# Second attention of a two-layer macaron block: scores in a ring of three pairs of banks, values two or three slots behind

## The chip, the cores and the metric

The kernel runs on one NeuronCore of one Trainium2 chip. The metric is device time in microseconds of one execution; lower is better. Engines are named as in the profile: PE is TensorE's matmuls (PEld its weight loads), DVE is VectorE, ACT is ScalarE, POOL is GpSimd, SP is the engine whose queue issues all DMAs. They run at the same time and meet at semaphores.

## What is computed

The input is 8 sequences of 512 tokens by 128 features. Two layers, each a feed-forward mixture of experts, an attention, and the same feed-forward again. The change touches the second layer's attention:

```python
def kernel_func(q, k):
    scores = jnp.einsum('bhqd,bhkd->bhqk', q, k) / jnp.sqrt(jnp.asarray(HD, q.dtype))
    w = jax.nn.relu(scores)
    return w / (jnp.sum(w, axis=-1, keepdims=True) + KERN_EPS)
...
qkv = (x @ w_qkv).reshape(Bx, Sx, H, 3 * HD)
...
attn = kernel_func(q, k)
out = jnp.einsum('bhqk,bhkd->bhqd', attn, v)
...
out = out @ w_out + b_out
y = x + out
```

There are 16 heads of 8 features. There is no mask and no exponential: the weights are relus, divided by their sum. A layer norm over the features of y ends it. The attention's input `x` is itself a layer norm of the running x, and what comes out is added to the running x.

## The kernel before, in words

Everything is float32 (or float32r, split in a high and a low part where three products replace one). The program runs six stages (`STAGES`): ffn0, attn0, ffn0, ffn1, attn1, ffn1. Each takes the eight sequences, called blocks here (`Chunk` in the code), one after the other; the first and the last block are written out, the six between are one loop body. A block has slots: 16 in attn1 (`NS1`). The order on every engine is written by hand. In each slot `run` issues first the steps of the block before that are left (`TAIL`: half, fin, aT_hi, aT_lo, proj, y_norm, y_rstd, y_scale, y_add), then steps that prepare the next block (`PREP`: the layer norm, its turn on PE, hi and lo; `QKV_AT`: keep, q, q_hi, q_lo, k, k_hi, k_lo, v, v_out), then the slot's own work. A number in these tables is the slot in which a step stands.

In attn1 a slot n is one group of four heads (quad, n // 4) and one block of 128 keys (n % 4). Its own work is:

- PE (`pe_attn1`, L753): four score matmuls (L763), one for each head of the quad. Each uses 24 rows of a strip of 32, so the four run beside each other. Each writes its own bank (0 to 3), 128 keys by 512 queries. Matmul j waits until the relu of slot n-1 for strip j is done (`p1_ready[j]`). Then come the four values matmuls of slot n-1 (`pv1`, L589, L598), float32, each to a strip of 32 output rows; the trace shows eight records for them. They add up over eight slots (two quads) in bank 5 for the first half of the heads and in bank 6 for the second.
- ACT (L881) and DVE (L1156) turn the scores into weights by a relu of 128x512 out of PSUM into the ring `probs` of three slots. ACT takes strips 0 and 1, and in slots 0, 2, 4, 6, 8, 10 strip 3 too; DVE takes the others.
- After eight slots the half of the output is turned and divided on DVE (`take_half`, L1063: L1075 transposes, L1081 adds the epsilon, L1083 takes the reciprocal, L1087 multiplies). The first half's stands in DVE's slot 9, ahead of the relus; the second half's in slot 1 of the next block.
- POOL copies the values into place (`put_values`, L1243), adds the last layer-norm bias to x (L1249, slot 10) and does the two steps of y_add (L1223, L1226), 128x512 each.
- SP writes q's and k's parts to DRAM (`write_stacks`) and reads them back for the four quads (`read_stacks`) in the layout of strips. A quad's buffers may be overwritten once its last score matmul of this block is done.

The steps that prepare the next block all use bank 7; the projection of the block before used bank 4 (`tail_bank`).

## Time and profile before

| | us |
|---|---|
| median of 3 runs | 2202.41 (2200.76 to 2204.6) |
| the profiled execution | 2207.97, its span 2206.2 |
| second attention in that span | 1484.0 to about 1812 |
| mean granted TensorE clock, whole span | 0.969 |

The profile is one execution. Its page gives the busy time of each engine, the trace behind it each instruction's start and duration, and what released an engine that had been idle. Matmul ends are modelled, so PE's busy time is read with care; starts are better. The granted clock is 1.00 at 2.4 GHz and 0.50 at 1.2 GHz; a stretch with both shows a mean.

### The profile page before, as it was taken

The page shows a single profiled execution, that of the slowest core. Times are in us where ns is not written, and L with a number is a line of the kernel's source. Part 1 is how long each engine was busy: PE and PEld are TensorE (multiplying, and loading weights), DVE is VectorE, ACT ScalarE, POOL GpSimd, SP SyncE. Part 2 cuts the span into 40 slices and gives each one's busy share as a digit, 9 for nine tenths or more (in the row PEclk, how much of TensorE's full clock was granted, in tenths as well). Part 3 has the DMA queues.
Part 4 walks back from the last instruction along what each step waited for, and adds up shares of the span by engine and source line. Part 5 has one row for each costly group of instructions (what it writes and reads, how often), then busy time and mean ns, then how long its engine had stood idle before and what let it go on. Part 6 is the DMA issues. An engine that isn't in the chain of part 4 may idle for free.

```text
span 2206.2 us, 45682 instructions
## 1 busy us (share of the span) xinstructions
PE 2073.0 (94%) x10800; PEld 1467.0 (66%) x10800; DVE 1683.5 (76%) x3458; ACT 1198.0 (54%) x1873; POOL 925.4 (42%) x904
## 2 busy tenths in 40 slices
PE   2999998999999899999999999999899899999999
PEld 2777776666666677777777777763333237777777
DVE  3777777777777577777588888876777777888887
ACT  3666664555555566666444444445555554444444
POOL 1655554323332456666444444440211214444444
PEclk9999998999999999999999999998889799999999
DMA  4333334233332234434211111123223201111112
GB/s 159 108 101 111 107 105 125 79 100 100 86 86 76 79 116 113 119 116 118 76 44 44 43 43 47 46 90 99 93 76 107 83 30 39 44 43 43 43 42 74
DMA packets 119983, 179.36 MB, mean 81 GB/s; under 512 B 33408, under 2 KB 37856, under 8 KB 119776
## 3 DMA queue, kind: packets, MB, share of 16 engines
q1 hardware_dynamic: 119904, 178.41, 27.0%
q8 instruction: 36, 0.59, 0.1%
q14 instruction: 43, 0.35, 0.0%
...
## 4 chain that ended last, share of the span: by engine, by line
PE 60%; issue 14%; POOL 11%; DVE 10%; ACT 2%; DMA 1%; SPq 1%; DVEq 1%; POOLq 1%; ACTq 0%
PE pair L382 12%; PE pair L384 11%; PE pair L383 11%; POOL h_lo L1282 9%; PE pair L763 4%; PE bank L598 3%; PE pair L598 3%; PE pair L683 3%; PE bank L584 3%; PE pair L705 3%; PE bank L382 1%; DVE rmax L1112 1%; PE bank L384 1%; PE bank L383 1%; DVE h_hi L1055 1%
## 5 line engine op out<-in xcount | busy, mean ns | idle before, releaser
L1288 POOL TENSOR_TENSOR h_lo<-hid,h_hi 128x512 fp32r<-128x512 f32 x256 | 333.7, 1303 | 441.5 <-ACT h_hi L852 441.4
L382 PE MATMUL pair<-xnT_hi,w_hi 128*128 (+1 forms) x1056 | 432.9, 410 | 1.1 <-DVE prod L1035 1.1
L1282 POOL TENSOR_TENSOR h_lo<-hid,h_hi 128x512 fp32r<-128x512 f32 x256 | 329.9, 1292 | 225.5 <-ACT h_hi L820 224.3
L384 PE MATMUL pair<-xnT_hi,w_lo 128*128 (+1 forms) x1056 | 418.4, 396 | 0.0
L383 PE MATMUL pair<-xnT_lo,w_hi 128*128 (+1 forms) x1056 | 416.2, 394 | 0.0
L847 ACT ACTIVATE hid<-pair,bias 128x512 f32<-128x512 f32 x256 | 176.3, 689 | 326.8 <-PE pair L384 323.0
L382 PE MATMUL pair<-h_hi,w_hi 128*128 128x512 f32 x784 | 318.3, 406 | 18.4 <-POOL h_lo L1282 8.9
L384 PE MATMUL pair<-h_hi,w_lo 128*128 128x512 f32 x784 | 309.5, 395 | 0.0
L383 PE MATMUL pair<-h_lo,w_hi 128*128 128x512 f32 x784 | 308.5, 394 | 0.0
L1055 DVE TENSOR_SCALAR h_hi<-pair,nb 128x512 fp32r<-128x512 f32 x256 | 191.1, 747 | 84.2 <-PE pair L384 83.2
L1035 DVE SCALAR_TENSOR_TENSOR prod<-pair,bias,wb 128x512 f32<-128x512 f32 x256 | 191.0, 746 | 67.0 <-PE pair L384 56.1
L870 ACT ACTIVATE probs<-pair 128x1024 f32<-128x1024 f32 x160 | 163.5, 1025 | 129.5 <-PE pair L705 126.1
L382 PEld LDWEIGHTS pair<-xnT_hi,w_hi 128*128 128x128 f32 x1056 | 199.9, 189 | 49.5 <-issue 6.1
L820 ACT ACTIVATE h_hi<-hid 128x512 fp32r<-128x512 f32 x256 | 161.2, 630 | 130.5 <-DVE hid L1040 126.2
L384 PEld LDWEIGHTS pair<-xnT_hi,w_lo 128*128 128x128 f32 x1056 | 199.2, 189 | 48.3
L881 ACT ACTIVATE probs<-pair 128x512 f32<-128x512 f32 x304 | 163.5, 598 | 121.3 <-PE pair L763 114.5
L383 PEld LDWEIGHTS pair<-xnT_lo,w_hi 128*128 128x128 f32 x1056 | 200.3, 190 | 39.1
L1040 DVE TENSOR_TENSOR hid<-pair,prod 128x512 f32<-128x512 f32 x256 | 177.1, 692 | 55.1 <-DVE prod L1035 35.7
L826 ACT ACTIVATE pair<-pair,bias 128x512 f32<-128x512 f32 x256 | 167.6, 655 | 72.6 <-PE pair L384 69.7
L1057 DVE SCALAR_TENSOR_TENSOR h_lo<-pair,nb,h_hi 128x512 fp32r<-128x512 f32 x256 | 192.2, 751 | 9.1
L1267 POOL TENSOR_SCALAR_AFFINE_SELECT probs<-probs 128x512 f32<-128x512 f32 (+1 forms) x160 | 86.9, 543 | 266.2 <-ACT probs L870 266.2
L382 PEld LDWEIGHTS pair<-h_hi,w_hi 128*128 128x128 f32 x784 | 147.8, 189 | 70.4 <-DVE h_lo L1057 11.3
...
## 6 DMA issues: line engine op xcount, KB each, us to landing
wb<-parts_dram SPq DMA_DIRECT2D x512, 128.0 KB, 2.9
wb<-parts_dram SPq DMA_DIRECT2D x128, 256.0 KB, 3.3
...
k_one<-parts_dram SPq DMA_DIRECT2D x128, 64.0 KB, 2.4
...
```

The costliest lines, as they stand in the source:

```text
L382: eng.matmul(o, w_hi_, v_hi, start=start, stop=False, **kw)
L383: eng.matmul(o, w_hi_, v_lo, start=False, stop=False, **kw)
L384: return eng.matmul(o, w_lo_, v_hi, start=False, stop=stop, **kw)
L826: eng.activation(gate_bank(p)[:, :] if p else gate[:, :], gate_bank(p)[:, :], ACT.Silu, bias=bias[:, b:b + 1]).then_inc(silu_ready, 1)
L847: eng.activation(hid[:, i % NHID, :], unit_bank(j)[:, :], ACT.Relu, bias=bias[:, B1 + j:B1 + j + 1]).then_inc(hid1_ready, 1)
L870: eng.activation(probs0[:, fill, :, :], pair[ring(("k", n))][:, :, :], ACT.Exp).then_inc(p0_full, 1)
L1035: eng.scalar_tensor_tensor(prod[:, p % 2, :], bank[2 + p % 2][:, :], bias[:, b:b + 1], wb[:, i % NWB, :], ALU.add, ALU.mult).then_inc(prod ...
L1040: eng.tensor_tensor(hid[:, i % NHID, :], gate_bank(p)[:, :], prod[:, p % 2, :], ALU.mult).then_inc(hid_ready, 1)
L1055: eng.tensor_scalar(h_hi[:, j % NH1, :], unit_bank(j)[:, :], floor, None, ALU.max).then_inc(hi1v_ready, 1)
L1057: eng.scalar_tensor_tensor(h_lo[:, j % NH1, :], unit_bank(j)[:, :], floor, h_hi[:, j % NH1, :].bitcast(F32), ALU.max, ALU.subtract).then_i ...
L1282: eng.tensor_tensor(h_lo[:, p % NH0, :], hid[:, unit_of(p) % NHID, :] if p else hs[:, :], h_hi[:, p % NH0, :].bitcast(F32), ALU.subtract). ...
L1288: eng.tensor_tensor(h_lo[:, j % NH1, :], hid[:, j // 2 % NHID, :], h_hi[:, j % NH1, :].bitcast(F32), ALU.subtract).then_inc(lo1p_ready, 1)
```

## The change

1. **Pairs.** The scores of a slot are now two pairs, m = 2n (strips 0 and 1) and 2n+1 (strips 2 and 3). Pair m is written to the two-bank tile `pair[m % 3]`, so banks 0 to 5 are a ring of three. A relu takes a whole pair, 128x1024. ACT takes each first pair, and in slots 0, 2, 10, 11, 13 (`ACT_BOTH`) the second too: 21 of 32. DVE takes 11. There is one counter for each of the two engines (`p1_ready`).
2. **Both waits, then four matmuls.** In slot n PE waits for the relus of the pairs three back, 2n-3 and 2n-2, and then issues the four score matmuls with no wait between.
3. **Values behind.** `PV_AT` lists which values steps stand in which slot. Slot 0 has step 13 of the block before, slot 1 its 14 and 15, slot 2 none, slot 3 steps 0 and 1, then n-2 up to slot 9, slot 10 none, and from slot 11 on n-3. All sums go to bank 6, so step 0 waits for the second half of the block before to be turned out of it, step 8 for the first half of this one. The ring of probs has four slots.
4. **Places.** half, fin, aT_hi, aT_lo move one slot back (2, 3, 4, 5), the first half's take from slot 9 to 10, the projection from 6 to 10 (now in bank 7), y_norm to 11, y_rstd 12, y_scale 13, y_add 14. q moves from slot 4 to 6, k from 5 to 7, v from 7 to 8, keep from 11 to 15. The layer norm's steps move by at most one slot, those of routing (last block) by up to two.
5. **Memory.** The larger probs ring lies over the buffer of the spread routing weights, so the loads for the stage after wait until the last values step (`pv1_done`); `attn1_xk` moves to buffers that only the first layer uses.

The core of the diff:

```diff
-    ("attn1", "attn1"): ((0, "pe", "pv_last"), (1, "dve", "half"), (2, "dve", "fin"), (3, "act", "aT_hi"),
-                         (4, "dve", "aT_lo"), (6, "pe", "proj"), (7, "dve", "y_norm"), (8, "pool", "y_rstd"), (9, "dve", "y_scale"), (10, "pool", "y_add")),
+    ("attn1", "attn1"): ((2, "dve", "half"), (3, "dve", "fin"), (4, "act", "aT_hi"), (5, "dve", "aT_lo"), (10, "pe", "proj"),
+                         (11, "dve", "y_norm"), (12, "pool", "y_rstd"), (13, "dve", "y_scale"), (14, "pool", "y_add")),
...
-    "attn1": (11, 4, 4, 4, 5, 5, 5, 7, 7),
+    "attn1": (15, 6, 6, 6, 7, 7, 7, 8, 8),
...
-HEAD_ORDER = (0, 2, 1, 3)
-ACT_THIRD = (0, 2, 4, 6, 8, 10)
+PV_AT = ((-3,), (-2, -1), (), (0, 1), (2,), (3,), (4,), (5,), (6,), (7,), (), (8,), (9,), (10,), (11,), (12,))
+ACT_BOTH = (0, 2, 10, 11, 13)
...
+def taken_by(m):
+
+    return "act" if m % 2 == 0 or m // 2 in ACT_BOTH else "dve"
...
             if kb == 0 and quad % 2 == 0:
-                eng.wait_ge(o_turned, 2 * ch.ga - 1 + quad // 2)
+                eng.wait_ge(o_turned, 2 * ch.ga + quad // 2)
+            for h in range(2):
+                eng.wait_ge(*taken_wait(ch, 2 * n + h))
             for j in range(QUAD):
-                eng.wait_ge(p1_ready[j], ROUND + i + 1)
-                ins = eng.matmul(bank[5 + quad // 2][PC * j:PC * (j + 1), :], mem1.v_st[:, kb, quad, j, :],
+                ins = eng.matmul(bank6[PC * j:PC * (j + 1), :], mem1.v_st[:, kb, quad, j, :],
...
-            for j in HEAD_ORDER:
-                rows_ = slice(PC * j, PC * j + NROW * HD)
-                eng.wait_ge(p1_ready[j], ROUND + i)
-                eng.matmul(bank[j][:, :], mem1.k_st[rows_, quad, kb * P:(kb + 1) * P], mem1.q_st[rows_, quad, :],
-                           start=True, stop=True).then_inc(s1_ps, 1)
-            if n:
-                pv1(eng, ch, n - 1)
+            for h in range(2):
+                m = 2 * n + h
+                if m >= NPAIR or not ch.first:
+                    eng.wait_ge(*taken_wait(ch, m - NPAIR if m >= NPAIR else max(k for k in range(NP1) if k % NPAIR == m) - NP1))
+            for h in range(2):
+                m = 2 * n + h
+                for j in range(2):
+                    rows_ = slice(PC * (2 * h + j), PC * (2 * h + j) + NROW * HD)
+                    ins = eng.matmul(pair[m % NPAIR][:, j, :], mem1.k_st[rows_, quad, kb * P:(kb + 1) * P], mem1.q_st[rows_, quad, :],
+                                     start=True, stop=True)
+                ins.then_inc(s1_ps, 1)
+            for m in PV_AT[n]:
+                if m >= 0:
+                    pv1(eng, ch, m)
+                elif not ch.first:
+                    pv1(eng, ch.before(), m + NS1)
...
+            elif before is not None and before.kind == "attn1":
+                eng.wait_ge(pv1_done, ROUND + NB * NS1)
```

How the order changes at three places of the middle blocks' body. ISA and REGISTER_ALU rows only wait or compute a semaphore's value. First PE, around the half. Before, the scores of slot 9 and the start of values step 8, with a wait at each matmul (pair0 and pair1 are banks 0 to 3):

```order
L763 MATMUL pair0<-attn1_q_st,attn1_k_st 128x512 [waits p1_ready0]
L762 ISA
L763 MATMUL pair1<-attn1_q_st,attn1_k_st 128x512 [waits p1_ready2]
L762 ISA
L763 MATMUL pair0<-attn1_q_st,attn1_k_st 128x512 [waits p1_ready1]
L762 ISA
L763 MATMUL pair1<-attn1_q_st,attn1_k_st 128x512 [waits p1_ready3]
L593 ISA
L595 ISA [waits v_put]
L597 ISA [waits o_turned]
L598 MATMUL bank6<-probs,attn1_v_st 32x512 [waits p1_ready0]
```

After, slots 10 and 11 (pair0 to pair2 are the ring; slot 10 has no values), up to the waits of values step 8:

```order
L777 ISA [waits p1_dve_ready]
L782 MATMUL pair2<-attn1_q_st,attn1_k_st 128x512 [waits p1_act_ready]
L782 MATMUL pair2<-attn1_q_st,attn1_k_st 128x512
L782 MATMUL pair0<-attn1_q_st,attn1_k_st 128x512 x2
L777 ISA
L777 ISA [waits p1_dve_ready]
L782 MATMUL pair1<-attn1_q_st,attn1_k_st 128x512 [waits p1_act_ready]
L782 MATMUL pair1<-attn1_q_st,attn1_k_st 128x512
L782 MATMUL pair2<-attn1_q_st,attn1_k_st 128x512 x2
L603 ISA
L607 ISA [waits v_put]
L609 ISA [waits o_turned]
```

The four waits became two, the values matmuls between the two slots' scores are gone, and the wait for the turned half stands ahead of step 8.

DVE at the same place. Before, slot 9, from the last op of y_scale to the last of the half (the relus of slot 9 follow it):

```order
L1199 TENSOR_SCALAR attn1_xk<-attn1_xk,y_mv,y_rstd 128x128
L1070 ISA
L1072 ISA [waits pv1_done]
L1075 STREAM_TRANSPOSE attn1_o_turn<-pair2 128x512 [waits attn_ready]
L1076 ISA
L1081 TENSOR_SCALAR rden<-attn1_o_turn 128x32 [waits o_turned]
L1082 ISA
L1083 RECIPROCAL rden<-rden 128x32 [waits eps_added]
L1084 ISA
L1086 REGISTER_ALU [waits rden_ready]
L1087 TENSOR_TENSOR attn1_attn<-attn1_o_turn,rden 128x16x16 [waits aT_ready]
```

After, slot 10, from the relu of slot 9 on; y_norm of slot 11 follows:

```order
L1180 TENSOR_SCALAR probs<-pair1 128x1024 [waits s1_ps]
L1094 ISA
L1096 ISA [waits pv1_done]
L1099 STREAM_TRANSPOSE attn1_o_turn<-bank6 128x512 [waits attn_ready]
L1100 ISA
L1105 TENSOR_SCALAR rden<-attn1_o_turn 128x32 [waits o_turned]
L1106 ISA
L1107 RECIPROCAL rden<-rden 128x32 [waits eps_added]
L1108 ISA
L1110 REGISTER_ALU [waits rden_ready]
L1111 TENSOR_TENSOR attn1_attn<-attn1_o_turn,rden 128x16x16 [waits aT_ready]
```

The half no longer follows y_scale; it stands between a relu and y_norm (L1210 and on), and no relu follows for two slots.

POOL in the middle body. Before, y_add (L1223, L1226), released by y_scale, and behind it the bias op L1249:

```order
L1221 ISA
L1223 ISA [waits tail_steps]
L1223 ISA
L1223 TENSOR_TENSOR attn1_xk<-attn1_xk,row 128x512
L1225 REGISTER_ALU [waits y_scaled]
L1226 ISA [waits x_biased]
L1226 ISA x2
L1226 TENSOR_TENSOR x<-x,attn1_xk 128x512
L1248 ISA
L1249 ISA [waits ln_steps]
L1249 ISA
L1249 TENSOR_TENSOR x<-x,row 128x512
```

After, from the bias op (now L1274) over a values copy and y_rstd to y_add (L1248, L1251):

```order
L1274 TENSOR_TENSOR x<-x,row 128x512
L1265 ISA
L1268 COPY attn1_v_st<-attn1_v_tok 128x4x4x8 [waits pv1_done]
L1244 TENSOR_TENSOR y_rstd<-y_ve,mhalf 128x4 [waits y_var]
L1246 ISA
L1248 ISA [waits tail_steps]
L1248 ISA
L1248 TENSOR_TENSOR attn1_xk<-attn1_xk,row 128x512
L1250 REGISTER_ALU [waits y_scaled]
L1251 ISA [waits x_biased]
L1251 ISA x2
L1251 TENSOR_TENSOR x<-x,attn1_xk 128x512
```

The bias op and the second values copy moved ahead of y_rstd; behind y_add there are only keep and one copy before the block ends.

## Rows read from the trace of the kernel before

**Rows 1.** Stretches: length; PE, PEld, DVE, ACT, POOL busy (count); clock, DMA, GB/s.

```profile
1484.00:1524.70 40.70, 37.17 (x215) 12.25 (x214) 25.02 (x52) 22.76 (x42) 4.36 (x6) 0.83 0.27 84
1524.70:1771.80 247.10, 227.48 (x1357) 81.41 (x1356) 181.62 (x397) 137.41 (x258) 49.40 (x60) 0.85 0.28 90
1771.80:1812.30 40.50, 36.70 (x224) 12.49 (x223) 30.69 (x84) 22.83 (x44) 6.25 (x6) 0.92 0.11 33
```

**Rows 2.** Groups of lines in one block, 1648.8 to 1688.4; busy, mean ns | idle.

```profile
L881 ACT ACTIVATE probs<-pair 128x512 f32<-128x512 f32 x38 | 20.4, 599 | 14.2 <-PE pair L763 14.2
L1156 DVE TENSOR_SCALAR probs<-pair 128x512 f32<-128x512 f32 x26 | 17.0, 685 | 6.3 <-PE pair L763 6.0
```

**Rows 3.** Timeline of PE in one block: start, us, engine, line, what, count.

```profile
1572.22 0.66 PE L512 MATMUL bank<-ident,xn 128*128 128x128 f32 x4
1572.80 0.50 PE L763 MATMUL pair<-attn_q_st,attn_k_st 24*128 24x512 f32 x4
...
1575.17 0.80 PE L763 MATMUL pair<-attn_q_st,attn_k_st 24*128 24x512 f32 x4
...
1580.71 0.51 PE L763 MATMUL pair<-attn_q_st,attn_k_st 24*128 24x512 f32 x4
...
1583.64 0.50 PE L763 MATMUL pair<-attn_q_st,attn_k_st 24*128 24x512 f32 x4
...
1588.83 0.50 PE L763 MATMUL pair<-attn_q_st,attn_k_st 24*128 24x512 f32 x1
1591.91 1.24 PE L763 MATMUL pair<-attn_q_st,attn_k_st 24*128 24x512 f32 x3 [2.58 <-DVE probs L1156]
...
1594.94 0.80 PE L763 MATMUL pair<-attn_q_st,attn_k_st 24*128 24x512 f32 x4
...
1597.53 0.80 PE L763 MATMUL pair<-attn_q_st,attn_k_st 24*128 24x512 f32 x4
...
1599.86 0.50 PE L763 MATMUL pair<-attn_q_st,attn_k_st 24*128 24x512 f32 x4
...
1603.19 0.50 PE L763 MATMUL pair<-attn_q_st,attn_k_st 24*128 24x512 f32 x4
1603.63 2.53 PE L598 MATMUL bank<-probs,attn_v_st 128*32 128x512 f32 x16
1606.09 0.50 PE L763 MATMUL pair<-attn_q_st,attn_k_st 24*128 24x512 f32 x4
```

**Rows 4.** Timelines of DVE and of POOL around 1588 to 1592, same block.

```profile
1588.25 0.99 DVE L1081 TENSOR_SCALAR rden<-attn_o_turn 128x32 f32<-128x32 f32 x1
...
1589.76 1.50 DVE L1087 TENSOR_TENSOR attn_attn<-attn_o_turn,rden 128x256 f32<-128x256 f32 x1
1591.17 0.68 DVE L1156 TENSOR_SCALAR probs<-pair 128x512 f32<-128x512 f32 x1
...
1587.92 1.28 POOL L1223 TENSOR_TENSOR attn_xk<-attn_xk,row 128x512 f32 x1 [2.19 <-DVE attn_xk L1199]
1589.71 1.26 POOL L1226 TENSOR_TENSOR x<-x,attn_xk  x1 [0.51 <-POOL attn_xk L1223]
```

**Rows 5.** Stretches of the same block before, in and after a fall.

```profile
1589.30:1592.70 3.40, 0.81 (x4) 0.44 (x3) 3.28 (x5) 0.78 (x2) 2.99 (x4) 1.00 0.00 0
1592.70:1596.20 3.50, 3.50 (x17) 0.69 (x20) 0.83 (x2) 1.45 (x3) 1.14 (x1) 0.50 0.00 0
1599.50:1603.00 3.50, 3.50 (x28) 1.05 (x24) 2.61 (x5) 2.17 (x4) 0.29 (x1) 0.99 0.00 0
```

**Rows 6.** ACT's timeline, and 128x1024 ops of the first attention (groups by form).

```profile
1600.39 1.08 ACT L881 ACTIVATE probs<-pair 128x512 f32<-128x512 f32 x2 [0.95 <-PE pair L763]
...
L870 ACT ACTIVATE probs<-pair 128x1024 f32<-128x1024 f32 x17 | 17.4, 1025 | 14.3 <-PE pair L705 14.0
...
L1115 DVE TENSOR_REDUCE rmax<-pair 128x2 f32<-128x1024 f32 x7 | 8.6, 1222 | 2.6 <-PE pair L692 2.5
```

**Rows 7.** Timeline of SyncE's DMA queue, same block.

```profile
1583.24 0.34 SPq L1317 DMA_DIRECT2D attn_q_st<-parts_dram  x1
```

More of the change, by code:

```diff
@@ L183, in __init__, with taken @@
             self.rmax = sb("rmax", [P, 2, NT, QUAD], F32)
-        else:
-            self.xk = sb("attn1_xk", [P, 2, NT, D], F32)
-def act_heads(n):
-    return (0, 1, 3) if n in ACT_THIRD else (0, 1)
+def taken_by(m):
+    return "act" if m % 2 == 0 or m // 2 in ACT_BOTH else "dve"
+def taken(m, who):
+    return sum(taken_by(i) == who for i in range(m))
 def build(nc, x_in, w0, w1, wa, biases, bd3, rows, consts, out, scratch, mixed):
@@ L298, in build @@
         st_ready, p0_full, p0_masked, pv0_done = map(sem, ("st_ready", "p0_full", "p0_masked", "pv0_done"))
[L299 removed]
+        s1_ps, pv1_done = sem("s1_ps"), sem("pv1_done")
+        p1_ready = {"act": sem("p1_act_ready"), "dve": sem("p1_dve_ready")}
         o_turned, eps_added, rden_ready, attn_ready = map(sem, ("o_turned", "eps_added", "rden_ready", "attn_ready"))
@@ L435, in xs_of @@
             return x[:, bass.ds(ch.c * NT, NT), :]
-        def tail_bank(ch):
-            return bank[4] if ch.kind == "attn1" and not ch.last else bank7
         def gate_bank(k):
@@ L528, in pe_prep @@
                 eng.wait_ge(st.sem, ch.g * st.per + st.per)
+                if ch.first and ch.s and STAGES[ch.s - 1] == "attn1":
+                    eng.wait_ge(tail.sem, 13 * (NB - 2) + 1)
                 for t in range(NT):
@@ L587, in pv0, with taken_wait @@
             ins.then_inc(pv0_done, 1)
+        def taken_wait(ch, m):
+            who, back = taken_by(m % NP1), 0 if m >= 0 else 1
+            return p1_ready[who], ROUND + (ch.g - back) * taken(NP1, who) + taken(m % NP1 + 1, who)
         def pv1(eng, ch, n):
@@ L620, in pe_tail @@
             if step == "pv_last":
-                pv1(eng, ch, NS1 - 1)
+                for m in PV_AT[0] + PV_AT[1]:
+                    pv1(eng, ch, m + NS1)
             if step == "pv_2":
@@ L625, in pe_tail @@
                 eng.wait_ge(aT_lo_ready, ch.ga + 1)
-                if ch.kind == "attn1" and not ch.last:
-                    eng.wait_ge(x_done, ONE + ch.G)
+                if ch.kind == "attn1" and isinstance(ch.c, int) and ch.c == NB - 2:
+                    eng.wait_ge(aff_ready, ch.gf + 1)
                 elif ch.last or ch.causal and isinstance(ch.c, int) and ch.c == NB - 2:
@@ L877, in act_attn1 @@
             eng.wait_ge(pv1_done, ROUND + i - PRING + 1)
-            for j in HEAD_ORDER:
-                if j in act_heads(n):
-                    eng.wait_ge(s1_ps, i * QUAD + HEAD_ORDER.index(j) + 1)
-                    eng.activation(probs[:, n % PRING, j, :], bank[j][:, :], ACT.Relu).then_inc(p1_ready[j], 1)
+            for m in (2 * n, 2 * n + 1):
+                if taken_by(m) == "act":
+                    eng.wait_ge(s1_ps, ch.g * NP1 + m + 1)
+                    eng.activation(probs[:, n % PRING, 2 * (m % 2):2 * (m % 2) + 2, :], pair[m % NPAIR][:, :, :], ACT.Relu).then_inc(
+                        p1_ready["act"], 1)
         def dve_prep(eng, step, ch):
@@ L1070, in take_half @@
                 eng.wait_ge(pv1_done, ROUND + ch.g * NS1 + (2 * half + 2) * NT)
-                src = bank[5 + half]
+                src = bank6
             eng.wait_ge(attn_ready, n)
@@ L1152, in dve_attn1 @@
             eng.wait_ge(pv1_done, ROUND + i - PRING + 1)
-            for j in HEAD_ORDER:
-                if j not in act_heads(n):
-                    eng.wait_ge(s1_ps, i * QUAD + HEAD_ORDER.index(j) + 1)
-                    eng.tensor_scalar(probs[:, n % PRING, j, :], bank[j][:, :], 0.0, None, ALU.max).then_inc(p1_ready[j], 1)
+            for m in (2 * n, 2 * n + 1):
+                if taken_by(m) == "dve":
+                    eng.wait_ge(s1_ps, ch.g * NP1 + m + 1)
+                    eng.tensor_scalar(probs[:, n % PRING, 2 * (m % 2):2 * (m % 2) + 2, :], pair[m % NPAIR][:, :, :], 0.0, None,
+                                      ALU.max).then_inc(p1_ready["dve"], 1)
         def dve_tail(eng, step, ch):
@@ L1403, in dma_body @@
                         read_stacks(eng, after, g)
-            elif after is not None and after.kind[:4] == "attn":
+            if ch.kind != "attn0" and after is not None and after.kind[:4] == "attn":
                 write_stacks(eng, after)
```

38 lines of the change are left out of this document (21 added, 17 removed), and 2 rows, old and new, of the table PREP.

## Prediction

> **What bounds the kernel now.** The change touches the second attention alone, so I first cut the trace there. The table by stretches [rows 1] gives its three parts: the first block of 512 tokens 40.7 us, the six in the middle 247.1 us (41.2 each), the last 40.5 us up to its last slot. The reader is to see that no engine is full in the middle ones: per block DVE is busy 30.3 us, ACT 22.9, POOL 8.2. PE reads 37.9, but its granted clock is 0.85 there, and its records are long where it waits. So the block is set by how the engines hand over to each other, and by the clock. The groups of lines [rows 2] say what is handed over: 38 relus of 128x512 on ACT (20.4 us) and 26 on DVE (17.0 us, 685 ns each).
>
> Then the timeline of PE, read by the starts of L763, the four score matmuls of a slot [rows 3]. A slot's PE work at full clock is short: scores at 1603.19, values from 1603.63, so 0.43 us for scores; two values steps and the loop's end take the 2.46 us up to 1606.09, so about 1.0 us for a values step and 0.4 for the branch. A slot needs 1.45 us of PE, the slot with q 2.37 (1572.80 to 1575.17), the one with v 2.93 (1580.71 to 1583.64). Over a block that is 16x1.45, plus 0.6 for the turn (1572.22 to 1572.80), 2x0.9 for q and k, 2x1.35 for v and the projection: 28.3 us of 41.2. The rest is in few places. Scores 10 begin at 1588.83 with one strip; the other three wait until 1591.91, released by DVE's relu, and the next slot starts at 1594.94: 6.1 us for one slot. The reason is in the rows of DVE and POOL [rows 4]: DVE takes the first half's output between two of its relus; its 128x32 op L1081 takes 0.99 us while POOL's L1223 runs, and its L1087 1.50 us, ending 0.28 us after POOL's L1226. After such a stall the granted clock is 0.50, its level of 1.2 GHz, against 1.00 before (PE was busy 0.81 us of the 3.4 ahead of the fall [rows 5]), and slots take 2.59 us (1594.94 to 1597.53) until it is back.
>
> The Trainium skill, SBUF — State Buffer, section "Who interferes with whom", says that a DVE instruction in a two-port mode or with two SBUF inputs shares a port with GpSimd and that the second one blocks. By that rule the trace agrees: 0.99 and 1.50 us, while the relu at 1591.17, which reads PSUM, takes its usual 0.68 though POOL works beside it.
>
> **The change, part by part.**
>
> *Scores in three pairs.* Before, a strip's scores n+1 wait for that strip's relu n, and each engine does two or three relus in a row, so the fourth strip waits for the second or third relu. After, scores n+1 wait for pair 2n (always ACT's) and pair 2n-1 (a slot older). The loop is: score start to relu start, relu, relu end to next scores. The first is 0.53 us (1599.86 on PE, 1600.39 on ACT [rows 3, 6]). The relu of 128x1024 isn't in this stage; the nearest row is ACT's 128x1024 exponential out of the same pairs, 1025 ns [rows 6]. Bounds: 0.96 (two of the 0.48 by which ACT's relus follow each other, 1.08 us for two [rows 6]) to 1.20 (two of 599 ns). I take 1.03, since shape and source are the same. The hand-back I take as 0.05 (DVE's relu ends at 1591.85 [rows 4], the scores that waited for it start at 1591.91). Together 1.61 us per plain slot, against PE's 1.45.
>
> *Relus.* Back to back, ACT's 38 at 0.48 are 18.2 us; the new 21 at about 0.90 (1.03 less the same overlap of 0.12) are 19.0, with its other ops of about 3 us 22. DVE goes from 17.0 to 11 of 128x1024; the nearest row is its maximum over the same shape, 1222 ns [rows 6]; two relus of now are 1.37, and below the maximum I know no row: 13.4 us, so 30.3-17.0+13.4 = 26.7, less 2.2 if the blocked ops of [rows 4] run free. Both stay under the 32 us below.
>
> *Values two or three slots behind, four probs buffers.* The PE work is the same 16 steps, but no values step waits for the newest relu, and in slots 2 and 10 PE runs none, so the half can leave bank 6 meanwhile. If that cover is gone, values wait for the transpose of 0.7 us and the relus before it. Slots 1 and 3 have two steps and cost 0.43+2.0 = 2.43 each.
>
> *The half moved to slot 10, y_add to slot 14.* On DVE, slots 10 and 11 (and 0, 2, 13) have no relu any more, so half, y_norm and y_scale stand where ACT takes both pairs. POOL's two 1.27 us ops now stand behind y_scale of slot 13, when DVE does relus out of PSUM. The x+bias op L1249 comes right after v, at my count 0.8 us ahead of the half.
>
> *q, k, v, later by two slots or less.* q to lo_cut to k: by cut durations of 0.6 and 0.7 us (ACT, DVE) k can start 1.5 us after q's end, about what scores and one values step take. SP's queue moves with it: its first stack read is at 1583.24 [rows 7], 8 us after q's scores slot began at 1575.17, so some 4 us after k's cut. In the new block k is cut about half way (16 of 32 us), so the first stacks are in by 24 us and are needed at 32. Hidden; the cover is 8 us. The loads of the next stage's weight rows now wait for the last values; their first user is 7 slots on. Hidden.
>
> **The sum, at full clock.** Starts of scores 0 to 15 and the next 0, each the later of PE's queue and the relu loop: 1.61, 2.43 (two values), 1.61, 2.43 (two values; turn and hi beside them), 1.61, 2.33 (q), 2.37 (k, waits q_lo), 2.91 (v, waits k_lo), 1.66 (v_out ahead of the relu), 2.78 (projection), 1.61, 1.81 and 1.82 (ACT has both pairs of 10 and 11), 1.62, 1.80 (both of 13), 1.60: 32.0 us, plus 0.3 of the branch that the loop doesn't cover: 32.3. By the same split the block of [rows 3] has 13.7 us in slots 4 to 9 against 13.7, 11.0 against 5.2 in 10 to 12, 6.2 against 5.3 in 13 to 15, and the rest against 8.1 in 0 to 3. So most of the gain is the stall and the half clock behind it.
>
> *The clock.* With eight score and sixteen values records in 3.5 us it stays at 0.99 to 1.00 [rows 5]. The new block has no stretch as empty as 0.81 of 3.4 us; the two free steps leave PE idle some 0.7 and 1.1 us. I count one short spell at half clock in a block, 1.5 us: 33.8. Bounds: none (32.3) and what the trace has now: a mean of 0.85 is 30% of the time at half speed, where the block's work, 52 us by rival 3, runs at 0.62 of the pace: 36.4.
>
> Middle blocks: 247.1-6x33.8 = 44.3. First block: it starts at half clock after the hand-over and has no tail work in it: 40.7 to 35, 5.7. Last: routing in place of q, k, v: 40.5 to 35, 5.5. At the exit three values steps stand ahead of the next stage in place of one: +1.5. Together 54 us of the profiled execution's 2207.97 (span 2206.2, and nothing around it changes), so 2154 there; the median of the runs is 5.6 lower, 2202.41, which gives **2148 us**.
>
> The Trainium skill, TensorE: Matmul & The Clock Gate, section "A second HAM failure mode: psum-queue depth-cycling", tells of a kernel that cycles PSUM banks, idles PE briefly between groups and so keeps falling back to the slow clock. This speaks against the change, and is the third rival. The trace bears it out only behind longer idle times.
>
> **Rivals.**
> 1. *The loop is longer than 1.61.* If scores in effect wait for the DVE pair too (0.53+1.22+0.05 = 1.80 each) and DVE's side work (half, fin, lo, aT_lo in slots 2 to 5) pushes that pair back, eight plain slots cost 0.2 to 0.5 more and slots 3 to 5 one us each: 36.5 to 37. Gain 6x4.5+8 = 35: 2167. For it: DVE is 80% full there. Against: its pair has a slot of slack.
> 2. *No change that can be told.* The clock losses of now (36.4), the relu at 1.20 (16x0.17 = 2.7) and the stall merely moved (POOL's bias op beside the half, 2 us): 41 us a block, about 2200.
> 3. *Slower: the clock stays low.* At half speed a slot is 2.59 [rows 3]; with q and k at 1.8 each, v and projection at 2.7 each and turn at 1.2 that is 52 us a block. A share f of the time at half speed makes it 32.3/(1-0.38f): the break-even of 41.2 is f = 0.57. At 0.75 it is 45 a block, 2202+8x4 = 2234. Against: PE's load rises to 28.3 of 33 us, and the clock held under such a load in [rows 5].
> 4. *Better:* clock full and 32.3 in all blocks: 2137.
>
> **Chances.** Forecast 0.55 (2141 to 2158), better 0.14, rival 1 0.23, rival 2 0.03, rival 3 0.05. The range leaves out rivals 2 and 3 and the ends of the better case: 2134 to 2173. A change under 0.2% can't be told from none in a measurement of this kernel; so faster 0.93, same 0.02, slower 0.05.
>
> **What would show it.** Right: blocks of 33 to 34.5 us; plain slots of 1.6 to 1.7; the relus near 1.03 and 1.22; L763's successor never waiting 2 us for DVE; L1081 and L1087's successors at their short times in slot 10; stage clock above 0.93. Wrong: blocks above 36 with score matmuls released by DVE; a clock under 0.85 in a stage without stalls; values waiting for the half (o_turned) in slot 3 or 11; scores waiting for a stack's DMA at slot 0.

## The result, and the profile after

The changed kernel takes **2153.65 us** (median of 4 runs, 2147.16 to 2157.78). The kernel before takes 2203.51 us beside it (4 runs, 2200.76 to 2208.39). The ratio is 0.9769, 95% interval 0.9738 to 0.9799: 50 us less, where the forecast was 2148 and the range 2134 to 2173.

The profiled execution took 2147.16 us, its span is 2145.4 and its mean granted clock 0.987. It is 6.5 us below the median of its runs; the profiled one of before is 4.5 above the median of its own. So the two spans lie 60.8 us apart and the medians 49.9. What follows explains the 60.8 of the traces, and comes back to the difference.

The stretches of the second attention, cut at the same places as [rows 1] (length; busy PE, PEld, DVE, ACT, POOL with counts; clock, DMA share, GB/s). The last one ends with the last values step, where the next stage's first matmul starts:

```profile
1484.70:1519.60 34.90, 28.60 (x195) 9.15 (x194) 20.52 (x33) 22.48 (x25) 4.35 (x6) 0.85 0.28 92
1519.60:1715.50 195.90, 174.54 (x1357) 60.28 (x1358) 150.38 (x308) 138.16 (x156) 48.87 (x59) 0.99 0.36 113
1715.50:1750.80 35.30, 31.32 (x244) 10.01 (x244) 26.18 (x72) 22.81 (x27) 6.93 (x8) 0.95 0.05 16
```

The middle went from 247.1 us to 195.9, its clock from 0.85 to 0.99. Of before, the last stretch to the same event is 1771.8 to 1811.5:

```profile
1771.80:1811.50 39.70, 35.90 (x221) 11.82 (x220) 29.99 (x83) 22.83 (x44) 6.25 (x6) 0.91 0.09 28
```

The rest adds nothing: from there to the span's end it is 2206.2-1811.5 = 394.7 us before and 2145.4-1750.8 = 394.6 after, and up to the stage it is 0.7 more. So 5.8 + 51.2 + 4.4 - 0.7 = 60.7 us, all of the difference of the spans.

A single middle block with no spell at half clock lasts 32.5 us, one with such a spell 33.3:

```profile
1552.10:1585.40 33.30, 30.31 (x230) 10.19 (x230) 25.07 (x52) 23.12 (x26) 8.56 (x11) 0.95 0.36 110
1585.40:1617.90 32.50, 28.84 (x227) 9.99 (x228) 25.02 (x52) 23.01 (x26) 8.03 (x11) 1.00 0.36 113
```

Groups of lines in the second of them, which answer to [rows 2] and [rows 6]. L904 is now ACT's relu, L1180 DVE's, L1105 and L1111 what L1081 and L1087 were:

```profile
L904 ACT ACTIVATE probs<-pair 128x1024 f32<-128x1024 f32 x21 | 20.5, 1027 | 6.2 <-PE pair L782 6.2
L1180 DVE TENSOR_SCALAR probs<-pair 128x1024 f32<-128x1024 f32 x11 | 13.4, 1217 | 4.0 <-PE pair L782 4.0
L782 PE MATMUL pair<-attn_q_st,attn_k_st 24*128 24x512 f32 x65 | 8.6, 495 | 4.0 <-ACT probs L904 2.9 <-DVE probs L1180 0.7
...
L1111 DVE TENSOR_TENSOR attn_attn<-attn_o_turn,rden 128x256 f32<-128x256 f32 x2 | 0.8, 424 | 0.2
L1105 DVE TENSOR_SCALAR rden<-attn_o_turn 128x32 f32<-128x32 f32 x2 | 0.4, 189 | 0.1
```

Both of DVE's ops of the half stand at their short times, 189 and 424 ns, and the scores wait 0.7 us for DVE in the whole block. The timeline of PE in the same block answers to [rows 3]: slots 4 and 5 (1593.33, 1594.95), then 10, 11 and 12 (1607.30, 1608.91, 1610.74). L782 is the scores, L611 the values:

```profile
1593.33 0.50 PE L782 MATMUL pair<-attn_q_st,attn_k_st 24*128 24x512 f32 x4
1593.76 1.06 PE L611 MATMUL bank<-probs,attn_v_st 128*32 128x512 f32 x8
1594.95 0.51 PE L782 MATMUL pair<-attn_q_st,attn_k_st 24*128 24x512 f32 x4
...
1607.30 0.51 PE L782 MATMUL pair<-attn_q_st,attn_k_st 24*128 24x512 f32 x4
1608.91 0.51 PE L782 MATMUL pair<-attn_q_st,attn_k_st 24*128 24x512 f32 x4 [1.11 <-ACT probs L904]
1609.35 1.07 PE L611 MATMUL bank<-probs,attn_v_st 128*32 128x512 f32 x8
1610.74 0.50 PE L782 MATMUL pair<-attn_q_st,attn_k_st 24*128 24x512 f32 x4 [0.33 <-ACT probs L904]
```

A plain slot is 1.62 us, by the starts of the scores. The four score matmuls always go together, and no slot is near the 6.1 us of [rows 3]. What PE waits for there is ACT: 0.33 us in slot 11, where ACT takes both pairs, 1.11 us in slot 10, which has no values. DVE and POOL at the same place, which answer to [rows 4]:

```profile
1606.11 0.71 DVE L1099 STREAM_TRANSPOSE attn_o_turn<-bank 128x512 f32<-128x512 f32 x1
1606.85 0.19 DVE L1105 TENSOR_SCALAR rden<-attn_o_turn 128x32 f32<-128x32 f32 x1
...
1604.00 1.27 POOL L1274 TENSOR_TENSOR x<-x,row 128x512 f32 x1
...
1613.97 1.28 POOL L1248 TENSOR_TENSOR attn_xk<-attn_xk,row 128x512 f32 x1 [2.18 <-DVE attn_xk L1224]
```

POOL's bias op has ended at 1605.27, 0.8 us ahead of the half, and y_add starts at 1613.97, long after it. The first stack read of the block stands in SyncE's queue at 1605.36, 20 us into the block, where [rows 7] had its own 18 us into it:

```profile
1605.36 0.34 SPq L1342 DMA_DIRECT2D attn_q_st<-parts_dram  x1
```

No score matmul of slot 0 waits for it.

### The profile page after: what moved, and what is told of

It reads as the page before. It is cut to its first block, busy times and chain, and to the rows that moved or that the text cites. A ratio compares the mean times of both kernels' runs of the same rounds, so it can differ in the third digit from the quotient of the medians.

```text
span 2145.4 us, 44900 instructions
## 1 busy us (share of the span) xinstructions
PE 2006.2 (94%) x10800; PEld 1441.4 (67%) x10800; DVE 1645.3 (77%) x3338; ACT 1197.4 (56%) x1737; POOL 925.7 (43%) x904
## 4 chain that ended last, share of the span: by engine, by line
PE 57%; issue 15%; POOL 12%; DVE 9%; ACT 5%; DMA 1%; SPq 1%; POOLq 1%; DVEq 0%; ACTq 0%
PE pair L389 12%; PE pair L391 12%; PE pair L390 12%; POOL h_lo L1307 9%; PE bank L611 3%; ACT probs L904 3%; PE pair L697 3%; PE pair L719 3%; PE bank L589 2%; PE pair L782 2%; PE bank L389 2%; DVE rmax L1136 1%; PE bank L391 1%; PE bank L390 1%; PE pair L706 1%
## 5 line engine op out<-in xcount | busy, mean ns | idle before, releaser
L893 ACT ACTIVATE probs<-pair 128x1024 f32<-128x1024 f32 x160 | 163.4, 1025 | 129.6 <-PE pair L719 126.3
L1081 DVE SCALAR_TENSOR_TENSOR h_lo<-pair,nb,h_hi 128x512 fp32r<-128x512 f32 x256 | 192.3, 751 | 9.1
L904 ACT ACTIVATE probs<-pair 128x1024 f32<-128x1024 f32 x168 | 164.6, 1026 | 59.6 <-PE pair L782 53.0
```

The lines of the kernel that those rows point to most:

```text
L904: eng.activation(probs[:, n % PRING, 2 * (m % 2):2 * (m % 2) + 2, :], pair[m % NPAIR][:, :, :], ACT.Relu).then_inc(p1_ready["act"], 1)
L1081: eng.scalar_tensor_tensor(h_lo[:, j % NH1, :], unit_bank(j)[:, :], floor, h_hi[:, j % NH1, :].bitcast(F32), ALU.max, ALU.subtract).then_i ...
```

## The experiments

Ten experiments: eight further kernels, and the changed kernel twice more (8 and 10). Each has runs of the kernel before beside it (medians 2202.6 to 2205.4). The changed kernel's own medians are 2153.65, 2152.03 (experiment 8) and 2153.11 (10); differences against it are taken from these. "Slot" lengths are differences of the starts of the score matmuls.

**1. The half and y_add alone.** The kernel before, with y_scale in slot 13 (it was 9), y_add in 14 (10) and keep in 15 (11), so that POOL's two ops no longer meet the half.

```diff
-... (8, "pool", "y_rstd"), (9, "dve", "y_scale"), (10, "pool", "y_add")),
+... (8, "pool", "y_rstd"), (13, "dve", "y_scale"), (14, "pool", "y_add")),
-    "attn1": (11, 4, 4, 4, 5, 5, 5, 7, 7),
+    "attn1": (15, 4, 4, 4, 5, 5, 5, 7, 7),
```

> The kernel before with one thing moved: y_scale from slot 9 to 13, y_add from 10 to 14 and, behind it on POOL, keep from 11 to 15. Four single score banks, values one slot behind and the half in slot 9 stay. Theory A (the loss in slots 9 to 12 was DVE's half standing behind y_scale and beside POOL's y_add, and the half clock behind it): L1081 at 0.19 us and L1087 at 0.42 in slot 9, the gap of PE before the last three score matmuls of slot 10 falls from 2.6 us to under 1, the clock no longer falls there, blocks of 36 to 37.5 us in place of 41.2, 25 to 35 us off the program. Theory B (the ring of pairs is what matters, places are secondary): blocks of 40 to 41, under 8 us off.

Measured: 2183.47 us (2179.35 to 2185.96), ratio 0.9901, interval 0.9879 to 0.9923: about 22 us below before, short of theory A's 25 to 35, though the blocks are as long as it said. DVE and PE in slot 9 and 10 of a block at full clock:

```profile
1658.15 0.19 DVE L1081 TENSOR_SCALAR rden<-attn_o_turn 128x32 f32<-128x32 f32 x1
...
1658.85 0.43 DVE L1087 TENSOR_TENSOR attn_attn<-attn_o_turn,rden 128x256 f32<-128x256 f32 x1
...
1658.79 0.50 PE L763 MATMUL pair<-attn_q_st,attn_k_st 24*128 24x512 f32 x1
1659.93 1.09 PE L763 MATMUL pair<-attn_q_st,attn_k_st 24*128 24x512 f32 x3 [0.65 <-DVE probs L1156]
```

The two ops fell from 0.99 and 1.50 us to 0.19 and 0.43, the wait ahead of the three scores from 2.58 to 0.65, and slot 10 from 6.1 to 3.2 us. A middle block is 37.1 us in the mean (222.6/6), with a clock of 0.94 in place of 0.85:

```profile
1523.00:1745.60 222.60, 213.64 (x1361) 80.47 (x1360) 169.88 (x398) 136.65 (x258) 49.40 (x60) 0.94 0.31 99
```

The edit also takes y_scale away from DVE's place ahead of the half, so a second cause has to be ruled out: that the half merely stood behind y_scale. The transposes that open the half, first before, then here, rule it out:

```profile
1587.50 0.72 DVE L1075 STREAM_TRANSPOSE attn_o_turn<-pair 128x512 f32<-128x512 f32 x1
...
1657.40 0.72 DVE L1075 STREAM_TRANSPOSE attn_o_turn<-pair 128x512 f32<-128x512 f32 x1 [1.03 <-PE pair L598]
```

Slot 9's scores start at 1587.25 before and at 1657.16 here, so the half starts 0.25 and 0.24 us behind them. Here DVE has been idle for 1.03 us and waits for the values. What differs is the two ops beside POOL: together 1.87 us longer before, and the wait ahead of the three scores 1.93 us longer.

So the meeting of DVE and POOL is the cause of the stall, and of much of the half clock behind it. It is less than half of the gain: a block at full clock is still 35.6 us here and 32.5 in the changed kernel. Nor was all the half clock of before behind this stall. In the block of [rows 3] the clock fell once more, behind slot 0, and there PE had waited only 0.68 us:

```profile
1566.61 1.48 PE L763 MATMUL pair<-attn_q_st,attn_k_st 24*128 24x512 f32 x4 [0.68 <-ACT probs L881]
...
1565.40:1568.80 3.40, 2.72 (x17) 1.23 (x16) 3.17 (x11) 2.56 (x5) 1.28 (x2) 1.00 0.21 78
1568.80:1572.20 3.40, 3.40 (x17) 0.55 (x12) 3.00 (x8) 1.80 (x4) 0.00 (x0) 0.50 0.00 0
```

Of some 72 us at half clock in the middle stretch of before, some 48 stand behind slot 10's stall and 24 behind slots 0 and 1. In this experiment they are 17 and 10: the clock still falls behind slot 10 in four of the six blocks, where theory A had it that it no longer does.

**2. The scores wait for the newest pair too.** The changed kernel with one more wait ahead of the scores of slot n, for the second relu of slot n-1. This takes away the slack of the ring and nothing else.

```diff
+            if n or not ch.first:
+                eng.wait_ge(*taken_wait(ch, 2 * n - 1))
```

> The changed kernel with one more wait: the scores of slot n also wait for the relu of the newest pair, 2n-1, as a ring two pairs deep would. Theory A (the slack of one slot hides DVE's other work, rival 1 of the prediction): plain slots rise from 1.62 to about 1.85 where DVE has nothing else, to 2.5 where ACT has both pairs, and in slots 1 and 3, where DVE's relu ends 3.4 to 3.7 us after the scores, to 3.5 and more; blocks of 40 to 42 us, 55 to 75 us more than the changed kernel, so the time of the kernel before. Theory B (the gain came from the places, the ring's third pair is worth the 0.2 us a slot of a longer relu): blocks of 34 to 35.5, 12 to 25 us more.

Measured: 2210.76 us (2206.28 to 2213.77), ratio 1.0021, interval 1.0010 to 1.0032: 57 us above the changed kernel, and above before too. A plain slot is 1.87 us. Slots 0, 2 and 10 are 2.53 and slots 11 and 13 are 2.8, since in these five ACT does both relus one behind the other and the scores wait for the second. PE, then ACT:

```profile
1651.71 0.51 PE L784 MATMUL pair<-attn_q_st,attn_k_st 24*128 24x512 f32 x4
...
1654.23 0.51 PE L784 MATMUL pair<-attn_q_st,attn_k_st 24*128 24x512 f32 x4 [1.02 <-ACT probs L906]
...
1652.24 1.94 ACT L906 ACTIVATE probs<-pair 128x1024 f32<-128x1024 f32 x2 [0.91 <-PE pair L784]
...
1530.20:1772.60 242.40, 199.35 (x1360) 63.66 (x1360) 152.26 (x308) 141.23 (x156) 49.85 (x60) 0.87 0.29 91
```

ACT and DVE are busy about as long as in the changed kernel (141.2 and 152.3 us against 138.2 and 150.4), but the middle stretch is 242.4 us in place of 195.9. The shortest block is 39.1 us and the longest 40.9; part of that is half clock, which is back at a mean of 0.87. Slots 1 and 3 came out shorter at full clock (2.69 and 2.29) than the 3.5 expected. So without the slot of slack the wider relus, the new places and the values behind gain nothing over before. The wait for a pair that is a slot old is what the gain stands on, with the relus shared out as they are. That condition matters: in the shortest block (39.1 us, 6.6 above a block of the changed kernel at full clock) the five slots in which ACT takes both pairs make up 4.9 of the 6.6. Scores that wait for the newest pair, with the relus shared out to suit that wait, were not run, so the 57 us are not the price of the ring's third pair in general.

**3. No free steps.** Values step 0 in slot 2 and 1 in slot 3; step 8 in slot 10 and none in slot 11.

```diff
-PV_AT = ((-3,), (-2, -1), (), (0, 1), (2,), (3,), (4,), (5,), (6,), (7,), (), (8,), (9,), (10,), (11,), (12,))
+PV_AT = ((-3,), (-2, -1), (0,), (1,), (2,), (3,), (4,), (5,), (6,), (7,), (8,), (), (9,), (10,), (11,), (12,))
```

> The changed kernel with values step 0 in slot 2 and 1 in slot 3 (before: none in 2, both in 3), and step 8 in slot 10, none in 11 (before: none in 10). Theory A (a free step pays only where the half is not yet turned when PE gets there): in slot 2 PE waits some 1.5 us for the turned half, slots 2 and 3 together take 5.2 us in place of 4.04; in slot 10 the half is turned (1606.82) before PE gets to the values (1607.73), so slots 10 and 11 stay at 3.45. In all 1.2 us a block, 8 to 11 us more. Theory B (both free steps are needed): 2 us a block or more, and a wait for the half in slot 10 too. Theory C (neither is needed): within 3 us.

Measured: 2164.75 us (2162.96 to 2168.23), ratio 0.9813, interval 0.9789 to 0.9837: 11 us above the changed kernel.

```profile
1560.96 0.51 PE L782 MATMUL pair<-attn_q_st,attn_k_st 24*128 24x512 f32 x4
1563.14 1.06 PE L611 MATMUL bank<-probs,attn_v_st 128*32 128x512 f32 x8 [1.68 <-DVE attn_o_turn L1099]
```

PE stands 1.68 us for the transpose of the half, behind xn and a relu on DVE. Slot 2 is 3.77 us in place of 1.62 and slot 3 is 1.67 in place of 2.42: 1.4 us a block, which makes 8.4 of the 11 us over six blocks; the rest goes with more half clock (slot 2 is 5.0 us in two blocks). Slots 10 and 11 stay at 1.62 and 1.83. There the projection stands ahead of the scores of slot 10 and makes slot 9 2.92 us long, 1.3 more than a plain one, and DVE's transpose runs beside it (1606.11 to 1606.82 above). The free step of slot 10 is not needed for the half.

**4. The projection in slot 11** (`proj_11`). If slot 10's free step leaves PE idle for 1.11 us, the projection can stand there.

```diff
-    ("attn1", "attn1"): (... (10, "pe", "proj"),
+    ("attn1", "attn1"): (... (11, "pe", "proj"),
```

> The changed kernel with the projection in slot 11 in place of 10, so that PE does its twelve matmuls (1.35 us) in the free step behind scores 10, where it waits 1.11 us for ACT. Theory A (PE's idle time in slot 10 can take it): slot 9 falls from 2.92 to 1.65, slot 10 rises from 1.62 to about 1.9; 1.0 us a block, 6 to 9 us less than the changed kernel. Theory B (y_norm, later by as much, pushes DVE's relu of slot 12 and the scores of 14): under 3 us less.

Measured: 2149.95 us (2145.79 to 2151.82), ratio 0.9748, interval 0.9727 to 0.9769: 2 to 4 us below the changed kernel, with runs that overlap its runs, so theory A's 6 to 9 did not come. Slots 9 and 10 are 1.62 and 1.92 us where they were 2.92 and 1.62: 1.0 us won, and slot 11 is 1.62 where it was 1.83. But slots 2 and 3 are 2.19 and 2.57, 0.7 lost, and in two blocks a spell at half clock stands there (3.9 and 4.3 us for slot 3):

```profile
1649.41 0.80 DVE L923 TENSOR_SCALAR ve<-mv 128x4 f32<-128x4 f32 x1
...
1653.18 0.65 PE L515 MATMUL bank<-ident,xn 128*128 128x128 f32 x4 [0.64 <-DVE xn L932]
```

y_norm, y_scale and so POOL's y_add and keep all come later, DVE's L923 now runs beside keep (0.80 us in place of 0.17; POOL's keep runs from 1648.91 to 1650.19), rstd starts behind it, and the turn of xn on PE waits 0.64 us.

**5. Relus of half the width.** Each relu of a pair as two of 128x512; the pairs, waits and order stay.

```diff
-                    eng.activation(probs[:, n % PRING, 2 * (m % 2):2 * (m % 2) + 2, :], pair[m % NPAIR][:, :, :], ACT.Relu).then_inc(
+                    eng.activation(probs[:, n % PRING, 2 * (m % 2), :], pair[m % NPAIR][:, 0, :], ACT.Relu)
+                    eng.activation(probs[:, n % PRING, 2 * (m % 2) + 1, :], pair[m % NPAIR][:, 1, :], ACT.Relu).then_inc(
```

> The changed kernel with each relu of 128x1024 as two of 128x512, the counter raised by the second. Ring, waits and places stay. Theory A (the width of a relu only sets the loop's length): on ACT 0.49+0.60 = 1.09 in place of 1.03, so plain slots 1.68 in place of 1.62 and slots where ACT has both pairs 2.0 in place of 1.83; 0.6 to 1.2 us a block, 5 to 10 us more. Theory B (the wide relu is what the gain rests on): blocks of 36 us and more, 25 us more.

Measured: 2159.51 us (2157.72 to 2163.06), ratio 0.979, interval 0.9766 to 0.9813: 6 to 7.5 us above the changed kernel. A plain slot is 1.68 us, one with both pairs on ACT 1.96 (1.83), a block at full clock 33.4.

```profile
1630.77 0.60 ACT L904 ACTIVATE probs<-pair 128x512 f32<-128x512 f32 x1 [0.84 <-PE pair L782]
1631.26 0.59 ACT L905 ACTIVATE probs<-pair 128x512 f32<-128x512 f32 x1
...
1631.90 0.51 PE L782 MATMUL pair<-attn_q_st,attn_k_st 24*128 24x512 f32 x4 [0.17 <-ACT probs L905]
```

Two narrow relus take 1.08 us from start to end (1630.77 to 1631.85), one wide 1.03: the 0.06 that a plain slot grew. The width is worth about a seventh of the 50 us.

**6. The bias op beside the half.** POOL's L1274 one slot later, in slot 11.

```diff
-            if slot == BIAS_AT:
+            if slot == (BIAS_AT if ch.causal else BIAS_AT + 1):
```

> The changed kernel with POOL's x+bias op (L1274, 1.27 us) in slot 11 in place of 10, so that it starts with the values copy behind it, beside DVE's half of slot 10. Theory A (the port is shared whatever the kernel, but here no relu stands behind the half): L1105 or L1111 in slot 10 takes up to 1.3 us in place of 0.19 and 0.42, y_norm ends up to 1.2 us later, and the slots of PE stay as they are: within 3 us of the changed kernel. Theory B (a blocked half costs its own length wherever it stands): 1 us a block, 6 to 10 us more.

Measured: 2150.06 us (2146.98 to 2153.68), ratio 0.9752, interval 0.9725 to 0.9778: no cost against the changed kernel, whose medians are 2152.0 to 2153.7.

```profile
1608.25 0.91 DVE L1105 TENSOR_SCALAR rden<-attn_o_turn 128x32 f32<-128x32 f32 x1
...
1607.84 1.28 POOL L1274 TENSOR_TENSOR x<-x,row 128x512 f32 x1
```

L1105 takes 0.91 us in place of 0.19 and ends at 1609.16, POOL's op at 1609.12. The first half of what [rows 4] showed is back: 0.72 us for L1105. L1111 keeps its 0.42, since only one op of POOL stands there and not two. PE's slots do not move (1.62, 1.83, 1.83). DVE has no relu in slots 10 and 11, and its relu of slot 12 starts 0.2 us later than in the changed kernel. So slots in which DVE has no relu hide a meeting of this size; whether they would hide the whole 1.87 us of before, with the distance to POOL's ops given up, was not run.

**7. The projection in slot 11 and y_scale in slot 12** (`proj_11_scale_12`). A try at mending 4.

```diff
-    ("attn1", "attn1"): (... (10, "pe", "proj"),
-                         (11, "dve", "y_norm"), (12, "pool", "y_rstd"), (13, "dve", "y_scale"), (14, "pool", "y_add")),
+    ("attn1", "attn1"): (... (11, "pe", "proj"),
+                         (11, "dve", "y_norm"), (12, "pool", "y_rstd"), (12, "dve", "y_scale"), (14, "pool", "y_add")),
```

> As proj_11, and y_scale in slot 12 ahead of DVE's relu in place of slot 13. In proj_11 the slots 9 and 10 gained 1.0 us, but POOL's chain y_add, keep, values copy, rstd ended 0.7 us later (rstd started 2.26 us into the block in place of 1.54), the layer norm's turn with it, and slots 2 and 3 gave 0.7 us back. Theory A (that chain starts with y_scale): rstd back at 1.54, slot 2 at 1.62, slot 3 at 2.42, blocks of 31.4 us where the clock is full; 6 to 9 us less than the changed kernel in all. Theory B (DVE's relu of slot 12, later by 1.2 us, holds the scores of slot 14): slot 13 above 2.2, nothing gained over proj_11.

Measured: 2158.32 us (2155.91 to 2158.6), ratio 0.9787, interval 0.9765 to 0.981. Slots 2 and 3 are 1.62 and 2.32 again, but slot 13 is 3.74 us:

```profile
1647.83 1.41 DVE L1224 TENSOR_SCALAR attn_xk<-attn_xk,y_mv,y_rstd  x4 [1.55 <-POOL y_rstd L1244]
1649.15 1.22 DVE L1180 TENSOR_SCALAR probs<-pair 128x1024 f32<-128x1024 f32 x1
...
1650.50 0.50 PE L782 MATMUL pair<-attn_q_st,attn_k_st 24*128 24x512 f32 x4 [2.24 <-DVE probs L1180]
```

The relu of slot 12 is now queued behind y_scale, which waits 1.55 us for POOL. Like the loss of before in slot 10, it is a relu behind side work on DVE; here the side work waits for a result of POOL, there it ran beside POOL's ops. The kernel is 5 to 6 us above the changed one, and theory B held.

**8. The changed kernel once more,** for the spread between executions.

> The changed kernel unchanged, to see how far its execution with a profile is typical: the one shown ran in 2147.2 us at a mean clock of 0.987, the others at 0.980 to 0.983 in 2153 to 2158. If the clock is the difference, this profile has the same slots of 1.62, 1.83, 2.3 to 3.0 us, and 2 to 5 more spells at half clock in some stage, each worth about 1.5 us; if something else is, the slots themselves differ.

Measured: 2152.03 us (2148.81 to 2153.3), ratio 0.9755, interval 0.9731 to 0.978. The slots at full clock are the same to 0.02 us in four of six middle blocks. The other two are 35.5 and 34.3 us, with half clock in slots 11 to 15, where the first profile had one such block (33.3). Its span is 2150.3 and its clock 0.984, against 2145.4 and 0.987.

**9 and 10. ACT takes slot 12's second pair in place of slot 13's,** with the projection in slot 11 (`proj_11_both_12`), and the changed kernel beside it.

```diff
-    ("attn1", "attn1"): (... (10, "pe", "proj"),
+    ("attn1", "attn1"): (... (11, "pe", "proj"),
-ACT_BOTH = (0, 2, 10, 11, 13)
+ACT_BOTH = (0, 2, 10, 11, 12)
```

> The projection stands in slot 11 as in proj_11, and ScalarE takes both relus of slot 12 instead of those of slot 13, so that VectorE has no relu between y_norm and y_scale. Theory A (what proj_11 lacked was the start of y_scale on VectorE: it stood behind the relu of slot 12, so that GpSimd's y_add, keep, copy and rstd all came 0.7 us late and the first slots of the next block waited): y_scale starts as soon as GpSimd's y_rstd is done, rstd starts about 1.5 us into the next block as in the changed kernel, slots 2 and 3 are 1.62 and 2.42 us again, slots 9 and 10 stay 1.62 and 1.92; a block is 31.4 us at full clock against 32.5, and the kernel 6 to 9 us below the changed one. Theory B (VectorE's relu of slot 13 now stands behind y_scale and ends late, as in proj_11_scale_12): the scores of slot 14 or 15 wait 0.5 to 1.5 us for it, a block is 32 to 33 us, and the kernel is within 3 us of the changed one or above it.

> The changed kernel unchanged, on the same chip and in the same rounds as proj_11_both_12. Both theories: the slots as in its profile (a block 32.5 us at full clock) and a median of 2148 to 2155 us; it tells what a difference of 3 to 6 us between the two is worth.

Measured: 2144.31 us (2143.17 to 2147.7), ratio 0.9719, interval 0.9699 to 0.9739, against 2153.11 us (2147.23 to 2154.4) of the changed kernel, ratio 0.975, interval 0.9728 to 0.9772. So 8.8 us less, the size that theory A gave, but only partly by its way. Slots 9 and 10 are 1.62 and 1.92, slot 2 is 1.64; but slot 3 is 2.57, slot 14 is 1.91 and slot 15 is 2.18 (1.83 and 1.87 before, theory B's cost). A block is 32.1 us, 0.4 less and not 1.1. The rest is the clock: the six middle blocks of the one and of the other are

```profile
1523.20:1715.80 192.60, 173.53 (x1360) 60.21 (x1360) 151.25 (x308) 138.63 (x156) 48.02 (x58) 1.00 0.36 115
...
1523.00:1722.90 199.90, 180.22 (x1356) 61.12 (x1356) 150.27 (x307) 138.42 (x156) 48.86 (x59) 0.96 0.35 110
```

7.3 us, of which 6x0.4 = 2.5 are the slots and 4.8 the half clock in three blocks of the second (34.4, 33.3, 34.6 against 32.5). Ahead of one of these falls, and behind it, the stretches of the changed kernel read

```profile
1612.80:1616.20 3.40, 1.97 (x20) 0.50 (x20) 2.54 (x11) 3.01 (x4) 0.08 (x1) 1.00 0.80 263
1616.20:1623.00 6.80, 6.80 (x36) 1.32 (x36) 3.14 (x6) 4.56 (x5) 3.65 (x4) 0.50 0.19 68
```

PE was busy 1.97 of 3.4 us, in which the free step of slot 10 falls. With the projection there it is busy 3.37 of 3.4 and then 3.06 of 3.5, and the clock stays:

```profile
1608.10:1611.50 3.40, 3.37 (x28) 1.96 (x28) 2.59 (x7) 2.83 (x3) 0.31 (x1) 1.00 0.85 268
1611.50:1615.00 3.50, 3.06 (x28) 0.70 (x24) 1.75 (x11) 3.50 (x5) 1.02 (x1) 1.00 0.59 190
```

In the changed kernel the same idle time stands in all six blocks and the clock fell behind it in one, two and three of them in three profiles. What decides between them stays open. That filling slot 10 keeps the clock up is what this profile without a fall in its middle blocks and the narrow range of five runs speak for. The profiles of experiments 4 and 7, which fill slot 10 too, agree: neither has a fall behind slot 10 in six blocks, only behind the waits in slot 2 (two blocks) and in slot 13. That makes none in 18 blocks, against six in the 18 of the three profiles of the changed kernel. In all of these traces a fall stands behind idle time of PE, but not every such idle time has a fall behind it.

## Why the prediction was right

The signs and the mechanism held, and the median fell in the forecast's own range (2141 to 2158). Step by step:

- **The loop.** Forecast 1.61 us for a plain slot, measured 1.62; relus 1.03 and 1.22, measured 1.027 and 1.217. That the maximum and the exponential of the first attention, taken as the nearest rows, cost just what the relus do was an assumption that held. The slots at full clock follow the list within 0.14 us each, but for slot 15, 1.87 against 1.60 (the 0.3 of the branch were added apart): 32.5 against 32.3 for a block. Slots 10 to 12 are 1.62, 1.83, 1.83 against 1.61, 1.81, 1.82. The largest other misses are 0.14 us: the projection's slot over, slot 1 under.
- **PE's own work** 28.8 us a block against 28.3, DVE 25.0 against 24.5, ACT 23.0 against 22.
- **The half.** L1105 and L1111 ran free as forecast, and experiment 1 shows the cause. The prediction put most of the gain there and on the half clock behind it; undone alone it gives 22 of 50 us. By experiment 2 the slack of a slot is worth 57 when all the rest is there. The two are taken from different ends, one from before and one from after, and are not a split of the 50. So the prediction's split is borne out only in part: more than half of the 50 needs the rest of the change, with the slack of the ring in it, though the prediction read the loop as a small gain beside the stall.
- **Free steps.** Right for slot 2 (1.4 us a block without it), wrong for slot 10: the projection covers the transpose there, and the free step costs 1.11 us of idle PE, and perhaps some of the clock (experiments 9 and 10).
- **Stacks and cover.** Read 20 us into the block, no wait.
- **The clock.** The mis-sized term. It was counted at 1.5 us a block, 9 for the six; in the three profiles it is 0.8, 4.8 and 4.8 in all six. The middle was put at 202.8 us and is 195.9 in the first of them. The prediction also read the trace of before as having falls only behind longer idle times, from the one behind 0.81 us of busy PE in 3.4. That reading is wrong: the same block has one behind 2.72 of 3.40 (experiment 1). It still counted a spell in every block, and six came in 18; why not more stays open.
- **First, last, exit.** First block 34.9 against 35. The last with the exit went from 39.7 to 35.3, 4.4 us, against 5.5-1.5 = 4.0. The two values steps more at the exit (three in place of one behind slot 15's own) cost 1.05 us where 1.5 was forecast, since from the last scores to the next stage it is now 1746.75 to 1750.76, 4.01 us, and was 1808.54 to 1811.50, 2.96.

The timeline of PE at the exit:

```profile
1746.75 0.51 PE L782 MATMUL pair<-attn_q_st,attn_k_st 24*128 24x512 f32 x4 [0.39 <-ACT probs L904]
1747.19 3.64 PE L611 MATMUL bank<-probs,attn_v_st 128*32 128x512 f32 x32
1750.76 0.50 PE L389 MATMUL pair<-xnT_hi,w_hi 128*128 128x512 f32 x1
```

The sum gave 54 us against a profiled execution that was 5.6 us slower than the median. The traces differ by 60.8 and the medians by 49.9. So the working was 7 us short between the profiles, nearly all of it clock, and the step to a median erred the other way: the profiled execution of after is a fast one, by the clock in its middle blocks (0.99, against 0.96 in experiment 10). The 54 us were counted from an execution of before that was 4.5 us slower than its median, and the forecast took all of them off the median too. From median to median it is 49.9, and that is most of why 2148 is 5.7 us too low. Against the other two profiles of the changed kernel (spans 2150.3 and 2151.7) the 54 would have been right within 2 us. So the median fell into the forecast's own range with some luck, since the two errors have opposite signs: the clock gave 7 us more between the traces than was forecast, and the medians lie 11 us less apart than the traces. The runs of before spread over 8 us and those of after over 11. Of the three profiles of the changed kernel, the spans differ by 6.3 us at most, and their middle blocks' half clock by 4.0.

Of the rivals, the first (scores that in effect wait for the newest pair) is what experiment 2 built; it priced a plain slot at 1.80 us, which is 1.87, and a block at 36.5 to 37, which is 39.1 to 40.9; it did not count what the slots cost in which ACT takes both pairs. In the changed kernel it doesn't happen. A term of the second, 2 us a block for POOL's bias op beside the half, was nothing in experiment 6. The third, a clock that stays low, did not come. The Trainium skill, TensorE: Matmul & The Clock Gate, section "A second HAM failure mode: psum-queue depth-cycling", tells of that result for kernels that cycle PSUM banks and idle in between. The trace agrees in that falls stand behind idle PE (1.97 of 3.4 us busy). It does not show a kernel that keeps falling: the middle blocks, with three pairs in turn, run at 0.99 and at 0.96 in experiment 10. The Trainium skill's rule in SBUF — State Buffer, section "Who interferes with whom", which the prediction drew on, fits three readings of the same op: 0.99 us beside POOL, 0.19 without (experiment 1), 0.91 when POOL's op is put back beside it (experiment 6).
